# A graph layer on one core: in the last phase's rounds ScalarE makes the mean, with counts from a column of ones

## The reference

```python
h = relu(layernorm(x))                                # 3125 x 64
msg = concat([h[dst], edge_attr])                     # 53125 x 128
e = relu(msg @ W1a.T + b1a) @ W1b.T + b1b             # hidden 128, out 64
sums, counts = segment_sum(e, src), segment_sum(1, src)
agg = sums / maximum(counts, 1)
z = relu(concat([h, agg]) @ W2a.T + b2a) @ W2b.T + b2b
out = x + concat([z, h]) @ Wr.T + br
```

## Time and profile before

| | us |
|---|---|
| median of 3 runs (lowest, highest) | 605.11 (603.81, 607.5) |
| the profiled execution, its own time | 605.74 |
| its span | 604.0 |
| mean granted TensorE clock, share of full speed | 0.769 |
| busy: GpSimd / VectorE / TensorE / ScalarE | 419.8 / 360.7 / 359.1 / 100.1 |

### The profile page before, as it was taken

One profiled execution on the slowest core, in us unless ns is written; L12 is line 12 of the kernel. 1 busy time (PEld: TensorE's weight loads), 2 busy tenths in 40 slices (PEclk: granted clock), 3 DMA queues, 4 the chain that ended last, 5 costly groups with the idle time before them and its releaser, 6 DMA issues.

```text
span 604.0 us, 7425 instructions
## 1 busy us (share of the span) xinstructions
PE 359.1 (59%) x2348; PEld 330.8 (55%) x2348; DVE 360.7 (60%) x1263; ACT 100.1 (17%) x145; POOL 419.8 (70%) x443
## 2 busy tenths in 40 slices
PE   5535866885124438438484443481676828798775
PEld 4435766465124438438484443481576828697654
DVE  7659643445324538547575444482585937979895
ACT  3231511212022012012121220120221111100022
POOL 2777777777777777777777777777777777777000
PEclk9665965757577688687698775875986977989998
DMA  8983845544345496686683646966867594959511
GB/s 199 357 229 94 238 142 153 165 110 129 93 126 174 144 295 198 192 273 198 197 261 103 184 154 201 292 175 203 245 223 262 157 301 135 308 185 330 177 44 55
DMA packets 54636, 116.33 MB, mean 193 GB/s; under 512 B 9869, under 2 KB 30949, under 8 KB 54593
## 3 DMA queue, kind: packets, MB, share of 16 engines
q1 hardware_dynamic: 41281, 85.11, 46.7%
q0 software_dynamic: 13312, 30.70, 16.3%
HBM read 68.62 MB, written 47.14 MB: 192 GB/s over the span
## 4 chain that ended last, share of the span: by engine, by line
POOL 44%; issue 18%; PE 15%; DVE 10%; DMA 7%; SPq 3%; ACT 2%; POOLq 0%; DVEq 0%; ACTq 0%
POOL slots_dram L413 44%; PE bank L916 6%; PE bank L900 6%; DMA slots_dram<-pay,pos_i 4%; DVE oh L528 3%; DMA dstb<-in_dst 2%; ACT pay L771 1%; PE bank L989 1%; DMA rows<-slots_dram 1%; DVE eo L517 1%; PE bank L866 1%; SPq L320 1%; SPq L272 1%; SPq L317 1%; ACT z1T L819 1%
## 5 line engine op out<-in xcount | busy, mean ns | idle before, releaser
L413 POOL DMA_INDIRECT slots_dram<-pay,pos_i x416 | 415.4, 999 | 137.1 <-issue 122.5
L900 PE MATMUL bank<-pw,eo 128*128 128x128 f32 x832 | 149.3, 354 | 197.4 <-DVE eo L517 196.6
L900 PEld LDWEIGHTS bank<-pw,eo 128*128 128x128 f32 x832 | 140.1, 263 | 206.9 <-issue 202.9
L916 PE MATMUL bank<-rows,oh 128*125 128x129 f32 x1050 | 134.5, 286 | 12.7 <-DVE oh L528 12.3
L916 PEld LDWEIGHTS bank<-rows,oh 128*125 128x125 f32 x1050 | 126.6, 197 | 17.9 <-issue 16.5
L771 ACT ACTIVATE pay<-bank 128x1024 f32<-128x1024 f32 x52 | 53.3, 1024 | 420.3 <-PE bank L900 419.2
L528 DVE TENSOR_SCALAR oh<-marks,rows 128x125 f32<-128x125 f32 x525 | 108.8, 294 | 1.5 <-DMA rows<-slots_dram 1.0
L506 DVE COPY pay<-mark 128x8 f32<-128x8 f32 x52 | 10.0, 195 | 148.5 <-DMA slots_dram<-pay,pos_i 147.9
L517 DVE TENSOR_SCALAR eo<-dstb,lane 64x256 f32<-64x256 int32 x208 | 64.9, 372 | 7.8 <-DMA dstb<-in_dst 7.0
L866 PE MATMUL bank<-we_in,hT 65*128 65x128 f32 x208 | 36.5, 334 | 0.7 <-ACT hT L756 0.7
L866 PEld LDWEIGHTS bank<-we_in,hT 65*128 65x128 f32 x208 | 34.9, 253 | 1.5 <-issue 1.1
(11 more groups left out here) (134 smaller groups left out, 174.0 us busy)
## 6 DMA issues: line engine op xcount, KB each, us to landing
rows<-slots_dram SPq DMA_DIRECT2D x24, 864.0 KB, 7.4
dstb<-in_dst SPq DMA_DIRECT2D x52, 256.0 KB, 7.0
eo<-in_edges_T SPq DMA_DIRECT2D x52, 256.0 KB, 3.8
rows<-slots_dram SPq DMA_DIRECT2D x12, 720.0 KB, 4.9
slots_dram<-zeros SPq DMA_DIRECT2D x9, 864.0 KB, 5.8
slots_dram<-pay,pos_i POOLq DMA_INDIRECT x416
rows<-slots_dram SPq DMA_DIRECT2D x8, 648.0 KB, 5.7
slots_dram<-zeros SPq DMA_DIRECT2D x3, 1008.0 KB, 6.8
```

The source lines that it names most:

```text
L413: pool.indirect_dma_start(out=slots_dram[:, :], out_offset=bass.IndirectOffsetOnAxis(ap=pos_i[:, u, k:k + 1], axis=0), in_=pay[:, u, k, :] ...
L900: last = T.matmul(bank[:, 2 * (g % 2) + k // 4, (k % 4) * HID:(k % 4 + 1) * HID], eo[:, u, k * 128:(k + 1) * 128], pw[:, g % WB, a, :], st ...
L916: last = T.matmul(o[0:BN, v * SW:(v + 1) * SW], oh2[:, r % 2, n, :], rows[:, sum_no[r] % RR, n, 0:SW], start=(t == 0), stop=(t == C[ph] - ...
```

## The change

ScalarE makes the mean in the tail rounds: up to three copies of 128 columns each, scaled by the reciprocal count, which VectorE still makes. The rows get a column ONE of ones behind the mark (SW = 130), so `sums` and `tot` hold the count itself in that column. VectorE's part becomes one max with 1.0 and a reciprocal. `rec_mark` goes (its iota on GpSimd, its reciprocal on VectorE); a memset of the ones is added on VectorE at the start. ScalarE's iteration becomes `mean(q)`, `mean_T(q-1)`, `relu_z(q-3)`. The wait for the transposes of round q-2, before `sbar` is written again, moves from VectorE to ScalarE, and `take_tail` gets a wait for the mean of round q-2, before `tot` is written again. The number of buckets in a round stays 3 (512 // 130).

```diff
--- before.py
+++ after.py
@@ -50,8 +50,8 @@
     assert all(0 < ROOM[ph] <= min(256, C[ph] * 128) for ph in range(NPH))
     BEGIN = [sum(C[:ph]) * NB * 128 for ph in range(NPH)]
     SLOTS = sum(C) * NB * 128
-    RW, SW = HID + 16, HID + 1
-    MARK = HID
+    RW, SW = HID + 16, HID + 2
+    MARK, ONE = HID, HID + 1
 
     X_PARTS = [(0, 2), (2, 9), (9, NB)]
     HALVES = [(0, 112), (112, BN)]
@@ -65,7 +65,7 @@
 
     sum_rounds = []
     for ph in range(NPH):
-        m = min(3, TPR // C[ph])
+        m = min(512 // SW, TPR // C[ph])
         for b0 in range(0, NB, m):
             sum_rounds.append(("sum", ph, b0, min(m, NB - b0)))
     tail_rounds = [v for v in sum_rounds if v[1] == NPH - 1]
@@ -117,7 +117,6 @@
         not_below = sb("not_below", [128, 128], bf16)
         ones_row = sb("ones_row", [1, 128])
         place = sb("place", [128, 1])
-        rec_mark = sb("rec_mark", [128, 1])
         marks = sb("marks", [128, BN])
         bucket_row = sb("bucket_row", [128, NQ])
         restart = sb("restart", [128, NQ, PK])
@@ -211,7 +210,7 @@
...
-            sb="mean_made", sT="mean_transposed", sTe="mean_T_evacuated", z="z_made", za="z_added", zr="z_relu",
+            rec="reciprocal_counts", sb="mean_made", sT="mean_transposed", sTe="mean_T_evacuated", z="z_made", za="z_added", zr="z_relu",
@@ -397,7 +396,6 @@
                             pattern=[[-1, 128]], channel_multiplier=1).then_inc(S["const"], 1)
             count(beyond[:], [[128 * K, PB], [128, K]], SLOTS, 1).then_inc(S["beyond"], 1)
             count(block_no[:], [[1, 2]], 0, 2)
-            count(rec_mark[:], [[0, 1]], 1, 1)
             count(marks[:], [[1, BN]], 1, 0).then_inc(S["const"], 1)
 
             pool.wait_ge(S["pad"], 1)
@@ -461,7 +459,8 @@
             V.memset(zeros[:], 0.0).then_inc(S["zero"], 1)
             V.memset(hT_all[:, 0:PAD_L], 0.0)
             V.memset(hT_all[:, PAD_L + N:PAD_L + N + PAD_R], 0.0).then_inc(S["hp"], 1)
-            V.memset(pay[:].rearrange("p u k w -> p (u k) w")[:, :, SW:RW], 0.0).then_inc(S["pad"], 1)
+            V.memset(pay[:].rearrange("p u k w -> p (u k) w")[:, :, SW:RW], 0.0)
+            V.memset(pay[:].rearrange("p u k w -> p (u k) w")[:, :, ONE:SW], 1.0).then_inc(S["pad"], 1)
             center(0)
             dve.wait_ge(S["ones"], 1)
             dve.wait_ge(S["lane"], 1)
@@ -525,7 +524,7 @@
                     dve.wait_ge(S["ag"], r - 1)
                 dve.wait_ge(s_rows[sum_no[r] % RR], loads_of_ring(r))
                 for t in range(m * C[ph]):
-                    last = V.tensor_scalar(oh2[:, r % 2, t, :], marks[:], rows[:, sum_no[r] % RR, t, MARK:SW], None, ALU.is_equal)
+                    last = V.tensor_scalar(oh2[:, r % 2, t, :], marks[:], rows[:, sum_no[r] % RR, t, MARK:ONE], None, ALU.is_equal)
                 last.then_inc(S["oh2"], 1)
 
             def summed(r):
@@ -608,8 +607,6 @@
                     make_h(1)
                     for ph in range(1, NPH):
                         limits(ph)
-                    dve.wait_ge(S["const"], 4)
-                    link(V.reciprocal(rec_mark[:], rec_mark[:]))
                 if i == 1:
                     center(2)
                     variance(2)
@@ -645,16 +642,13 @@
             def take_tail(q):
                 r, b0, m = tails[q]
                 dve.wait_ge(S["ag"], r + 1)
+                if q >= 2:
+                    dve.wait_ge(S["sb"], q - 1)
                 V.tensor_tensor(tot[:, q % 2, 0:m, :], sums[:, b0:b0 + m, :], summed(r), ALU.add).then_inc(S["tk"], 1)
                 dve.wait_ge(S["tk"], r + 1)
-                if q >= 2:
-                    dve.wait_ge(S["sT"], q - 1)
                 c = cnt[:, q % 2]
-                link(V.tensor_scalar(c[:, 0:m, 0], tot[:, q % 2, 0:m, MARK], rec_mark[0:BN, :], MAGIC, ALU.mult, ALU.add))
-                link(V.tensor_scalar(c[:, 0:m, 1], c[:, 0:m, 0], -MAGIC, 1.0, ALU.add, ALU.max))
-                link(V.reciprocal(c[:, 0:m, 2], c[:, 0:m, 1]))
-                V.tensor_tensor(sbar[:, q % 2, 0:m, :], tot[:, q % 2, 0:m, 0:HID], c[:, 0:m, 2].unsqueeze(2).to_broadcast((BN, m, HID)),
-                                ALU.mult).then_inc(S["sb"], 1)
+                link(V.tensor_scalar(c[:, 0:m, 0], tot[:, q % 2, 0:m, ONE], 1.0, None, ALU.max))
+                V.reciprocal(c[:, 0:m, 1], c[:, 0:m, 0]).then_inc(S["rec"], 1)
 
             def add_z(q):
                 r, b0, m = tails[q]
@@ -804,19 +798,36 @@
                 if g == 6:
                     late_weights()
 
-            for q in range(NJ + 2):
+            def mean(q):
+                r, b0, m = tails[q]
+                act.wait_ge(S["rec"], q + 1)
+                if q >= 2:
+                    act.wait_ge(S["sT"], q - 1)
+                for v in range(m):
+                    last = A.activation(sbar[:, q % 2, v, :], tot[:, q % 2, v, 0:HID], ACT.Copy, scale=cnt[:, q % 2, v, 1:2])
+                last.then_inc(S["sb"], 1)
+
+            def mean_T(q):
+                r, b0, m = tails[q]
+                act.wait_ge(S["sT"], q + 1)
+                if q >= 2:
+                    act.wait_ge(S["z"], q - 1)
+                A.copy(sbarT[:, q % 2, 0:m * BN], bank[:, 7, 0:m * BN]).then_inc(S["sTe"], 1)
+
+            def relu_z(q):
+                r, b0, m = tails[q]
+                act.wait_ge(S["za"], q + 1)
+                if q >= 2:
+                    act.wait_ge(S["o"], q - 1)
+                A.activation(z1T[:, q % 2, 0:m * BN], zt[:, q % 2, 0:m * BN], ACT.Relu).then_inc(S["zr"], 1)
+
+            for q in range(NJ + 3):
                 if q < NJ:
-                    r, b0, m = tails[q]
-                    act.wait_ge(S["sT"], q + 1)
-                    if q >= 2:
-                        act.wait_ge(S["z"], q - 1)
-                    A.copy(sbarT[:, q % 2, 0:m * BN], bank[:, 7, 0:m * BN]).then_inc(S["sTe"], 1)
-                if q >= 2:
-                    r, b0, m = tails[q - 2]
-                    act.wait_ge(S["za"], q - 1)
-                    if q >= 4:
-                        act.wait_ge(S["o"], q - 3)
-                    A.activation(z1T[:, q % 2, 0:m * BN], zt[:, q % 2, 0:m * BN], ACT.Relu).then_inc(S["zr"], 1)
+                    mean(q)
+                if 1 <= q <= NJ:
+                    mean_T(q - 1)
+                if 3 <= q:
+                    relu_z(q - 3)
 
             act.wait_ge(S["flag"], 1)
             is_bad = act.value_load(flag[0:1, 0:1], min_val=0, max_val=1)
...
```

More of the change, by code:

```diff
@@ L722, in _ @@
                         dve.wait_ge(L["oe"], b)
-                    step(V.tensor_scalar(cnt[:, 0, 0, 1:2], sums[:, b, MARK:SW], 1.0, None, ALU.max))
+                    step(V.tensor_scalar(cnt[:, 0, 0, 1:2], sums[:, b, MARK:ONE], 1.0, None, ALU.max))
                     step(V.reciprocal(cnt[:, 0, 0, 2:3], cnt[:, 0, 0, 1:2]))
-                    step(V.tensor_scalar(cnt[:, 0, 0, 3:4], sums[:, b, MARK:SW], 0.5, None, ALU.is_lt))
+                    step(V.tensor_scalar(cnt[:, 0, 0, 3:4], sums[:, b, MARK:ONE], 0.5, None, ALU.is_lt))
                     V.tensor_scalar(sbar[:, 0, 0, :], sums[:, b, 0:HID], cnt[:, 0, 0, 2:3], None, ALU.mult).then_inc(L["mean"], 1)
```

## The result

The changed kernel takes 611.87 us in the median of 4 runs (610.33 to 614.78), beside 606.20 for the kernel before in the same comparison (603.81 to 607.5). The ratio of the runs is 1.0153, with a 95% interval of 1.0101 to 1.0205: slower, clear of the noise, though whether by 2% stays open. The forecast was 611.7 us and slower. The median is there; the ratio, put on 606.2, gives 615.5, just beyond the upper end of the range (615.0). So the direction and the mechanism have to be looked at apart from the size.

What follows compares the result with a forecast made beforehand. GpSimd's scatters bound the kernel until the tail, where VectorE set the period; only the tail could pay. Tail +6.4 us and column 0.2 make +6.6 on 605.74, 612.3; the median lies 0.6 lower, 611.7 us; range 607.5 to 615.0.

Steps and rivals of the forecast that it cites:

- VectorE sets the pace before, and loses 0.75 us of work per round: Tail rounds: VectorE's steps fill the 3.04 us period; the change cuts its own sum to 2.29 us.
- The loop through ScalarE's order, 4.53 us: Tail rounds: mean ahead of relu closes a loop through `outs` and VectorE's reciprocal; period goes from 3.04 to 4.53 us.
- A scaled copy: 0.40 us, 0.29 apart: ScalarE, tail: each mean copy takes 0.40 us and occupies 0.29, three 0.87; bounds 0.16 and 0.43 each.
- The ends of the range, +4.2 and +9.2 us: Tail: the closed loop's own ends by the copies' bounds; with 0 to 0.5 for the 130th column, 609.3 to 614.8 us.
- The first rounds escape: Tail's beginning: `outs` exists only from iteration 3, so the first `outs` comes at 579.79 us, against 579.88 before.
- The column costs 0.2 us; the waits that were moved cost nothing: 130th column: 0.2 us ahead of the tail, bounds 0 and 0.5; moved and new waits find their work done.
- The rival that VectorE sets the pace: Tail: period set by VectorE's 2.29 us or TensorE's order; tail ends 4.7 us earlier, 600.6 us; chance 0.06.
- TensorE's clock should hold: Tail: clock stays 1.00 at 60% busy; the rival, a fall, gives about 620 us; chance 0.05.
- the forecast +6.4: Tail: following the engines, the last addition ends at 605.1 us against 598.73, so +6.4 us.
- the likeliest case: Tail: the closed loop through ScalarE's order, with the clock held; chance 0.82, 607.5 to 615.0 us.
- +6.6 was forecast: Whole kernel: the sum of the tail's +6.4 us and 0.2 us for the 130th column.
- the signs of being wrong: `outs` period 3.0 or less, copy start-to-start outside 0.16 to 0.43, tail clock 0.50, tail beginning over 1 us from 570.3.

Runs made afterwards that it cites:

- three exchanges of the same instructions: Changed kernel with ScalarE's iteration reordered: mean, relu, copy (ratio 1.0111); copy, relu, mean (0.9970); relu, copy, mean (0.9905).
- the other order: Changed kernel with ScalarE's iteration as relu(q-3), transposed copy (q-1), mean(q); ratio 0.9905 to the kernel before, tail 23.31 us.
- the control: The changed kernel run again with nothing altered; ratio 1.0129 to the kernel before, tail 38.56 us.
- product twice: Changed kernel with the `z1` product of rounds 1 to 8 made twice into the same bank; ratio 1.0146, tail 35.68 us.
- three times: Changed kernel with the `z1` product of rounds 1 to 8 made three times into the same bank; ratio 1.0136, tail 36.47 us.
- copy, relu, mean: Changed kernel with ScalarE's iteration as transposed copy (q-1), relu(q-3), mean(q); ratio 0.9970, tail 26.38 us.
- the filled kernels: Changed kernel with the `z1` product of rounds 1 to 8 made twice or three times, giving TensorE more work; ratios 1.0146 and 1.0136.

## Why the prediction was right, and where it was not

- *VectorE sets the pace before, and loses 0.75 us of work per round.* Right: max and reciprocal take 0.17 and 0.18 us as L654 and L655 did. As forecast, it waits instead, 1.7 to 2.5 us per round for `outs`.
- *The loop through ScalarE's order, 4.53 us.* Right, 4.57 and 4.58 in the rounds with the clock at 1.00, and shown to be the order by three exchanges of the same instructions: 4.21, 2.89 and about 2.35 us, where following the engines had given 4.2, 2.89 and 2.4 to 2.5.
- *A scaled copy: 0.40 us, 0.29 apart.* Measured: 0.39 and 0.30. The estimate by the Trainium skill's figures ("ScalarE: Activation LUTs", section "What ACT_TABLE_LOAD costs") is 0.39 and 0.29 to 0.30, and the trace agrees. The ends of the range, +4.2 and +9.2 us, do not quite follow from the 0.19 us that each 0.01 us of a copy is worth; by that they are +3.9 and +9.1.
- *The first rounds escape.* Right: from the beginning of the tail to the first `outs` it was 9.58 us (before: 9.55; worked out: 9.46).
- *The column costs 0.2 us; the waits that were moved cost nothing.* Nothing contradicts it; the column is too small to be seen.
- *The rival that VectorE sets the pace, 600.6 us if the relu stood ahead.* It did not happen for the change as made, but for the other order its forecast held: 4.5 us less than before was worked out, and 597.5 us beside 602.94 was measured. Of the two bounds it named for that order it is TensorE's, not VectorE's.
- *TensorE's clock should hold; chance 0.05, all or nothing, some +8 us more.* This is the step that failed. I compared shares of busy time (1.18 of 2.00 us at 576 us in the earlier trace rows, 60% afterwards) and concluded that a like share keeps the clock. It did not: in the changed kernel the clock fell in one middle round and in the wind-down, in the control in two middle rounds and in most of the wind-down. It added 1.7 us to the forecast +6.4 in the one, and some 3.3 in the other (38.56 - 28.40 - 6.4, less the 0.5 of small terms). The row at 576 us stood for the tail's beginning only, as these rows show, two of the kernel before and one of the changed one:

```profile
572.00:580.00 8.00, 4.84 (x27) 3.05 (x27) 7.52 (x29) 1.83 (x4) 0.00 (x0) 1.00 0.42 110
585.70:588.74 3.04, 2.70 (x17) 1.96 (x18) 2.90 (x11) 0.89 (x2) 0.00 (x0) 1.00 0.00 0
...
576.86:581.43 4.57, 2.54 (x17) 1.94 (x17) 2.21 (x8) 1.76 (x5) 0.00 (x0) 1.00 0.07 16
```

Before, TensorE was busy 61% of the time in the first rounds and 89% in a full one (2.70 of 3.04 us); in the changed kernel a middle round has 56% (2.54 of 4.57 us), round after round. With hindsight the term belonged into the likeliest case, as 1.2 us for one round in three, with a range to 3 us above; the centre would then have been near 613.5, and 615.5 inside.

The sizes fit together. The ratio on 606.2 us is +9.3 us, and the two tails are 8.6 and 10.2 us longer, where +6.6 was forecast; most of what is missing is the clock's. That the median of 611.87 us lies on the forecast of 611.7 is luck. Two of the signs of being wrong showed: the clock of 0.50 in the tail, which is the failed step, and a tail that began 3.05 us away from 570.3, which is the scatter that the second profiles show.

## What to carry to other kernels

Before work is moved to an engine with much idle time, write down what will stand behind it in that engine's order, and follow the wait round: in this loop the instruction that needs the newest round's value had to stand behind the ones that finish old rounds. Exchanging three blocks of one loop here is worth 2 to 2.5% (1.0153 and 1.0129 against 0.9905) with not one instruction changed. And where a change makes TensorE wait in every round, add a term for its clock: where it fell here, a round of 4.57 us took 5.28 to 5.78.

## What was not expected of the hardware

In a tail in which TensorE is busy 56% of a middle round, its clock stayed at 1.00 in some rounds and fell to 0.50 in others, and in different ones from one execution to the next: once in the middle in one profile of the changed kernel, twice in the other. In the four profiles with falls the longest pauses of TensorE ahead of `outs` were 1.67 to 2.03 us; but in the control the first fall, at 579.6 us, came when the longest had been 1.53. In the profiles where the longest were 1.40 (product twice), 0.78 (three times) and 0.34 us (copy, relu, mean), the clock held. These seven profiles don't say which pause is too long, or whether it is the pause that decides and not the work between: the filled kernels had both shorter pauses and more work.
